# Dots of an attention stage on eight array tiles in two bursts, with maxima per batch and the pad dropped by the exp's bias

## The reference

```python
h = tok(x)                          # windows of 8 time points pooled by a softmax: (128, 94, 64)
h = h + attn(layernorm(h))
h = h + ffn(layernorm(h))           # routed experts, hidden size 128
# attn: 8 heads of 8 features, 94 queries and keys
dots = einsum('bhnd,bhmd->bhnm', q, k)
grass = einsum('bhnd,bhmd->bhnm', qr(q).Q, qr(k).Q) ** 2 * grassman_scale
a = concat([dots * scale, dots ** 2 * riem_scale, grass])      # 24 maps
a = conv_w @ batchnorm(a) + conv_b                             # 8 mixed maps
out = softmax(a, axis=-1) @ v                                  # then the projection
```

## Time and profile before

| | before |
|---|---|
| median of 3 runs | 1039.53 us (1038.96 to 1039.94) |
| profiled execution | 1039.8 us |
| its span | 1038.1 us |
| mean granted TensorE clock | 0.941 |
| PE busy | 919.1 us (89%) |
| DVE busy | 760.2 us (73%) |
| POOL busy | 500.9 us (48%) |
| ACT busy | 400.7 us (39%) |

### The profile page before, as it was taken

The page is one execution under the profiler, slowest core; times in us unless marked ns, Lnnn a source line. Parts: engine busy times, 40 slices in busy tenths (PEclk is TensorE's granted clock), DMA queues, the critical chain, the costliest instruction groups (busy, mean ns, idle before and its releaser), DMA issues. The chain is left out here.

```text
span 1038.1 us, 38252 instructions
## 1 busy us (share of the span) xinstructions
PE 919.1 (89%) x15147; PEld 599.2 (58%) x15147; DVE 760.2 (73%) x1336; ACT 400.7 (39%) x647; POOL 500.9 (48%) x567
## 2 busy tenths in 40 slices
PE   4677678998929999999999999999999998889995
PEld 2233245555626666666666666666666665557673
DVE  4588964887965888888888888888888888645552
ACT  2333422113604444444444444444444443224442
POOL 3355631110026666666666666666666663023440
PEclk8788888998968999999999999999999999889997
DMA  8665000325001111111111111111111110000111
GB/s 302 250 224 193 1 0 4 60 53 134 0 19 53 52 51 51 51 51 50 48 48 47 49 48 51 49 51 51 51 51 51 51 47 23 1 0 21 33 33 33
DMA packets 64446, 63.25 MB, mean 61 GB/s; under 512 B 37081, under 2 KB 55068, under 8 KB 64412
## 3 DMA queue, kind: packets, MB, share of 16 engines
q1 hardware_dynamic: 63884, 61.25, 20.1%
q10 hardware_dynamic: 528, 1.54, 0.4%
HBM read 52.93 MB, written 6.75 MB: 57 GB/s over the span
## 5 line engine op out<-in xcount | busy, mean ns | idle before, releaser
L1177 ACT ACTIVATE sq<-ps_dot 128x752 f32<-128x752 f32 x192 | 153.1, 797 | 302.5 <-PE ps_dot L1056 302.5
L1056 PE MATMUL ps_dot<-q_st,k_blk 32*64 32x94 f32 x6144 | 169.5, 247 | 3.0 <-POOL k_blk L1016 3.0
L1056 PEld LDWEIGHTS ps_dot<-q_st,k_blk 32*64 32x64 f32 x6144 | 134.4, 133 | 64.6 <-issue 50.0
L1016 POOL TENSOR_TENSOR k_blk<-k_turn,hmask 128x384 f32<-128x384 f32 x64 | 65.5, 1023 | 177.4 <-ACT k_turn L1165 177.4
L1224 DVE TENSOR_REDUCE sums<-prob 128x94 f32<-128x564 f32 x128 | 147.9, 1199 | 2.0 <-ACT prob L1170 2.0
L1020 POOL TENSOR_TENSOR k_mix<-k_cm,cols 128x768 f32<-128x768 f32 x64 | 119.9, 1873 | 0.0
L1002 POOL TENSOR_TENSOR v_blk<-v_rep,vmask 128x384 f32<-128x384 f32 x128 | 106.6, 854 | 6.8 <-PE ps_m L1088 6.8
L1105 PEld LDWEIGHTS ps_a<-q_st,k_mix 64*64 64x64 f32 x3072 | 77.2, 132 | 56.4 <-issue 48.2
L1105 PE MATMUL ps_a<-q_st,k_mix 64*64 64x94 f32 x3072 | 101.0, 250 | 0.8 <-DVE prob L1212 0.8
L1170 ACT ACTIVATE prob<-prob,cols 128x564 f32<-128x564 f32 x128 | 91.1, 758 | 20.4 <-DVE prob L1212 20.4
L1195 DVE TENSOR_REDUCE row_max<-ps_a 128x94 f32<-128x564 f32 x128 | 89.3, 741 | 12.4 <-PE ps_a L1124 12.4
(11 more groups left out here) (222 smaller groups left out, 1419.3 us busy)
## 6 DMA issues: line engine op xcount, KB each, us to landing
v_rep<-v_rows SPq DMA_DIRECT2D x256, 96.0 KB
x_g<-in_x_dram SPq DMA_DIRECT2D x15, 1500.0 KB, 6.6
v_rows<-tok SPq DMA_DIRECT2D x32, 96.0 KB
q_st<-q_cm SPq DMA_DIRECT2D x64, 47.0 KB, 1.8
out_dram<-rows SPq DMA_DIRECT2D x16, 188.0 KB
x_g<-in_x_dram ACTq DMA_DIRECT2D x1, 1500.0 KB, 7.4
top_rows<-tok SPq DMA_DIRECT2D x16, 32.0 KB
top<-top_rows SPq DMA_DIRECT2D x1, 512.0 KB, 3.5
```

Source lines behind the costliest of these rows:

```text
L1016: return pool.tensor_tensor(k_blk[:, a, :, kind], view.unsqueeze(2).broadcast_to([128, NTAU, 4, 8]), k["hmask4"][:].unsqueeze(1).unsqueeze ...
L1056: mm = pe.matmul(ps_dot[64 * hg:64 * hg + 64, (a + g) % 2, b, col:col + N], k_blk[rows, a, 2 * (2 * g + t2) + mi].rearrange("p k h m -> p ...
L1177: act.activation(sq[:, :, :, 2 * g:2 * g + 2, :].rearrange("p mi b t n -> p b mi (t n)"), ps_dot[:, (a + g) % 2, :, 0:4 * N].rearrange("p ...
```

## The change

It does five things, all for `attend`.

1. The dots of mi = 1 go to the other column half (`at = 64 * (hg ^ mi)`), so that eight different 32x64 tiles of the array are used. There are two bursts of 24 matmuls; each fills all four banks of `ps_dot` (one for each batch and mi), three values of t a burst.
2. As the head groups of mi = 1 are now swapped on the partitions, `mix_w` has a second, swapped copy (four more small matmuls in `constants`).
3. The turned keys go to `ps_m`, no longer into `ps_dot`. The order on TensorE changes: both transpositions and both spreads of the maxima stand behind the key turn and ahead of the second burst. The second transposition waits for ScalarE's copy of the turned keys (the same bank). Batch 0 has its maxima in a free part of `ps_a`, batch 1 in `ps_m`.
4. ScalarE, no longer VectorE, adds the constant to the spread maxima (`shift_out`). Its queue is: key copy, two squares (one a batch), two shifts, exp of batch 0, two squares, exp of batch 1.
5. VectorE subtracts batch by batch over all six t. The pad keys of t = 5 are dropped by another bias in the exp (`pad_bias`), so each exp is two instructions, 470 and 94 columns. `sums` has two buffers.

```diff
@@ attend: TensorE
-                if later(i, 1) or g == 2:
-                    pe.wait_ge(s["squared"], 3 * i + g - 1)
-                for t2 in range(2):
+                if half or later(i, 1):
+                    pe.wait_ge(s["squared"], 2 * i + half)
+                for t3 in range(3):
                     for mi in range(2):
                         for b in range(2):
                             for hg in range(2):
                                 rows = slice(64 * b + 32 * hg, 64 * b + 32 * hg + 32)
-                                col = N * (2 * mi + t2)
-                                mm = pe.matmul(ps_dot[64 * hg:64 * hg + 64, (a + g) % 2, b, col:col + N],
-                                               k_blk[rows, a, 2 * (2 * g + t2) + mi].rearrange("p k h m -> p (k h m)"),
+                                at = 64 * (hg ^ mi)
+                                mm = pe.matmul(ps_dot[at:at + 64, b, mi, N * t3:N * t3 + N],
+                                               k_blk[rows, a, 2 * (3 * half + t3) + mi].rearrange("p k h m -> p (k h m)"),
                                                q_st[rows, a, :], start=True, stop=True)
...
             def step(i, a, has_prev, has_prev2, has_next):
                 dots(i, a, 0)
-                if has_prev:
-                    turn_max(i - 1)
-                dots(i, a, 1)
-                if has_prev:
-                    spread_max(i - 1)
-                dots(i, a, 2)
                 if has_next:
                     turn_keys(i + 1, 1 - a)
+                if has_prev:
+                    turn_max(i - 1, 0)
+                    if has_next:
+                        pe.wait_ge(s["kt_out"], i + 2)
+                    turn_max(i - 1, 1)
+                    for b in range(2):
+                        spread_max(i - 1, b)
+                dots(i, a, 1)
                 if has_prev2:
                     attended(i - 2, a, False)
-                    denominators(i - 2, i)
+                    denominators(i - 2, a, i)
@@ attend: ScalarE
+            def shift_out(prev, b):
+                act.wait_ge(s["max_spread"], 2 * prev + b + 1)
+                if later(prev, 1):
+                    act.wait_ge(s["sub_done"], 2 * (prev - 1) + b + 1)
+                act.activation(shift[:, b, :], max_bank(b, slice(0, 128), N), ACT.Identity, bias=k["conv_const"]).then_inc(s["max_out"], 1)
+
+            def exps(prev, a, b):
+                act.wait_ge(s["sub_done"], 2 * prev + b + 1)
+                act.activation(prob[:, a, b, 0:5], prob[:, a, b, 0:5], ACT.Exp, bias=k["conv_const"])
+                act.activation(prob[:, a, b, 5], prob[:, a, b, 5], ACT.Exp, bias=k["pad_bias"][:]).then_inc(s["exp_done"], 1)
...
@@ attend: VectorE
-                dve.tensor_scalar(shift[:].rearrange("p b n -> p (b n)"), ps_m[:, 0:N2], k["conv_const"], None, ALU.add).then_inc(s["shift_done"], 1)
...
-                dve.tensor_tensor(prob[:, a, :, 0:5, :], bass.AP(ps_a[:].tensor, A_AT, [[3 * 512, 128], [B_AT - A_AT, 2], [N, 5], [1, N]]),
-                                  shift[:].unsqueeze(2).broadcast_to([128, 2, 5, N]), ALU.subtract)
...
+                for b in range(2):
+                    dve.wait_ge(s["max_out"], 2 * prev + (b + 1))
+                    dve.tensor_tensor(prob[:, a, b], all_logits(b, [[N, NT], [1, N]]), shift[:, b, :].unsqueeze(1).broadcast_to([128, NT, N]),
+                                      ALU.subtract).then_inc(s["sub_done"], 1)
```

More of the change, by code:

```diff
@@ L229, in _ @@
             step(dve.tensor_tensor(k["hmask4"][:], k["hmask"][:, 0:4], k["hmask"][:, 4:8], ALU.add))
-            step(dve.tensor_scalar(k["pad_col"][:], k["delta"][:, 7:8], PAD_GAP, None, ALU.mult))
+            step(dve.scalar_tensor_tensor(out=k["pad_bias"][:], in0=k["delta"][:, 7:8], scalar=-PAD_GAP, in1=k["conv_const"],
+                                          op0=ALU.mult, op1=ALU.add))
             for b in range(2):
@@ L274, in _ @@
             pe.wait_ge(dve_step, marks["mix_rows"])
-            for quarter, source in enumerate((0, 2, 1, 3)):
-                mm = pe.matmul(ps_t[32 * quarter:32 * quarter + 32, 1, 256:320], k["ident"][:, 32 * source:32 * source + 32], mix_rows[:],
-                               start=True, stop=True)
+            for mi, order in enumerate(((0, 2, 1, 3), (1, 3, 0, 2))):
+                for quarter, source in enumerate(order):
+                    mm = pe.matmul(ps_t[32 * quarter:32 * quarter + 32, 1, 256 + 64 * mi:320 + 64 * mi],
+                                   k["ident"][:, 32 * source:32 * source + 32], mix_rows[:], start=True, stop=True)
             mm.then_inc(pe_step, 1)
@@ L957, in attend @@
         prob = sb("prob", [128, 2, 2, NT, N])
-        sums = sb("sums", [128, 2, N])
+        sums = sb("sums", [128, 2, 2, N])
         inv = sb("inv", [128, N])
@@ L1037, in turn_keys, with dots @@
                 pe.wait_ge(s["m_ready"], i + 1)
-                if later(i, 1):
-                    pe.wait_ge(s["squared"], 3 * i - 1)
-                pe.matmul(ps_dot[:, a, 0, KT_AT:KT_AT + NP], m_blk[:, a].rearrange("p q d -> p (q d)"), k_cm[:, span(i, 1), :],
-                          start=True, stop=True).then_inc(s["kt_done"], 1)
-            def dots(i, a, g):
-                if g == 0:
+                if later(i, 4):
+                    pe.wait_ge(s["out_done"], i - 3)
+                pe.matmul(ps_m[:, KT_AT:KT_AT + NP], m_blk[:, a].rearrange("p q d -> p (q d)"), k_cm[:, span(i, 1), :],
+                          start=True, stop=True, skip_group_check=True).then_inc(s["kt_done"], 1)
+            def dots(i, a, half):
+                if half == 0:
                     pe.wait_ge(q_in[a], 16 * ((i - a) // 2 + 1) if isinstance(i, int) else 8 * (i - a) + 16)
@@ L1151, in _ @@
             steps(pe, step)
-            turn_max(PAIRS - 1)
-            spread_max(PAIRS - 1)
+            for b in range(2):
+                turn_max(PAIRS - 1, b)
+            for b in range(2):
+                spread_max(PAIRS - 1, b)
             attended(PAIRS - 2, 0, False)
-            denominators(PAIRS - 2, None)
+            denominators(PAIRS - 2, 0, None)
             attended(PAIRS - 1, 1, True)
-            denominators(PAIRS - 1, None)
+            denominators(PAIRS - 1, 1, None)
         @block.scalar
@@ L1181, in step @@
                 if has_prev:
-                    exps(i - 1, 1 - a)
+                    act.wait_ge(s["mixed"], 2 * i)
+                for b in range(2):
+                    squares(i, 0, b)
+                if has_prev:
+                    for b in range(2):
+                        shift_out(i - 1, b)
+                    exps(i - 1, 1 - a, 0)
+                for b in range(2):
+                    squares(i, 1, b)
+                if has_prev:
+                    exps(i - 1, 1 - a, 1)
             turned_out(0, 0)
             steps(act, step)
-            exps(PAIRS - 1, 1)
+            for b in range(2):
+                shift_out(PAIRS - 1, b)
+            for b in range(2):
+                exps(PAIRS - 1, 1, b)
         @block.vector
```

133 lines of the change are left out of this document (61 added, 72 removed).

## The result

| | before | after |
|---|---|---|
| median of 4 runs each, same chip | 1039.66 us (1038.96 to 1039.94) | 1108.84 us (1105.61 to 1115.37) |
| ratio, 95% interval | | 1.0674 (1.0618 to 1.0731) |
| span of the profiled execution | 1038.1 us | 1104.1 us |
| mean granted TensorE clock | 0.941 | 0.879 |

A forecast was written before the change was run, and what follows sets the result against it. TensorE and VectorE were taken to hold each other in a ring of 8.85 us per step. The new ring through ScalarE summed to 8.46, −0.39 × 62 = −24 us, giving 1015.5 us, range 986 to 1054.

The forecast's parts named there:

- Nothing elsewhere. POOL's turned keys come earlier: POOL: turned keys come earlier, as the key copy ends near 1.4 us of a step, not 4.62; no cost added.
- copies stay: VectorE: copies of the head maxima unchanged, while its work per step falls from 7.4 to about 7.2 us.
- rival E: TensorE's clock falls during small instructions between dot bursts; a step of 9.4 us, +36, 1076 us; chance 0.06.
- the milder half of E: The part of the clock-fall rival counted inside the range: little time at the lower clock level.
- 0.45 us of gaps: TensorE's forecast idle time among five small instructions between 0.64 and 2.79 us of the new step.
- rival C: Eight tiles don't run at once: 0.02 us per pass stays, a burst is 1.13 us, 1069 us; chance 0.12.
- the pass time of a tile: TensorE: a matmul pass occupies its own tile for 0.09 us, however many tiles run beside it.
- the mis-sized term: Dots on TensorE: with six passes per tile, the next burst could start 0.64 us after the old one, not 0.81.
- TensorE's path: Chain beside the new ring, through second transposition, spreads, burst 2, attended and mixing, to 5.83 us; loses by 0.08.
- rival D: ScalarE's chain of nine instructions and five hand-overs is dearer, 0.03 us each; time stays, 1030 to 1044; chance 0.13.
- Rival B: The ring dissolves, engines slip past each other and VectorE's work alone bounds; −78, 962 us; chance 0.07.
- What would show it: Signs for the forecast: 48-pass bursts about 0.7 us, ScalarE start times, clock 0.98 or more; three signs against.

The follow-up runs named there:

- after_reduce: Changed kernel with VectorE's wide copy of the head maxima rewritten as a reduction over an axis of one element; 1028.19 us, ratio 0.9905.
- before_reduce: Kernel before with the wide copies of the head maxima written as reductions over one element, nothing else; 1045.92 us, ratio 1.0073.
- after_fill_small: Changed kernel, copies kept, plus four idle-time matmuls a step whose results go unused; 1048.53 us, ratio 1.0095.
- four_tiles: Changed kernel with the dots back on four of eight array tiles and both mixing weights alike; 1123.02 us, ratio 1.081.
- keys_late: Kernel before with the key turn moved behind attended and denominators, and its ScalarE copy behind the exps; 1113.36 us, ratio 1.0717.

## Why the prediction was wrong

**The step that failed** is "Nothing elsewhere. POOL's turned keys come earlier", with "copies stay" in the paragraph on VectorE. Both sentences were true of the order and false of the time. I had costed the move of the turned keys at nothing without naming what they would lie beside. All that was needed stood in reach: their new time (from 1.8 us of a step, behind `k_mix`, which ends 1.87 us into a step of before; the key copy was forecast to end at 1.4), their length (1.02), and the copies' new place (about 1.8 to 2.5). `after_reduce` shows the cause, one instruction rewritten for 80 us, and `before_reduce` that the rewritten form is no gain where no POOL instruction runs beside it.

**The clock, rival E,** was given 0.06 and 1076 us. Its mechanism is what made a loss of 11 us (`after_fill_small`) into one of 69, and at 60 us it is dearer than the 36 that I had worked out. The range let in only "the milder half of E", so the measured time fell out of it by this term. It was rated low because the forecast step had 0.45 us of gaps. With the held copy TensorE waited 0.31 + 0.64 = 0.95 us between the two bursts of each step, with the reduction 0.31 + 0.32 = 0.63, and the stage's clock was 0.88 and 1.00. So the chance of E hung on a size that I had taken as fixed. The price per disturbed step follows from the rows: attended burst to denominators 610.11 − 608.17 = 1.94 against 1.00, the second dot burst and the denominators 0.21 and 0.17 more, the mixing burst 0.06, in all 1.38. 60 us are thus about 43 such steps of 62, an estimate; the trace has 41 among its last 59. Two limits: `four_tiles` waited longer still (0.31 + 0.85 + 0.16) and kept 0.96, and `keys_late` waited 1.34 us in each step and kept 1.00, so the sum of the gaps alone doesn't tell the level; and why some steps of one kernel fall and others don't stays open.

**Eight tiles do run together;** rival C is refuted. The same burst cut after 0.35 us and whole, from two windows of the timeline of after:

```profile
643.98 0.58 PE L1068 MATMUL ps_dot<-q_st,k_blk 32*64 32x94 f32 x32
```
```profile
643.98 0.87 PE L1068 MATMUL ps_dot<-q_st,k_blk 32*64 32x94 f32 x48
```

The last of 32 passes starts by 644.33, so they start 0.35/31 = 0.011 us apart or less, half of before's 0.020. Cut earlier, the same timeline holds 8 passes by 644.04, 16 by 644.17 and 24 by 644.25: eight start nearly together, and behind the first sixteen the next eight come every 0.08 us, as the groups of four do in a burst of before. So the pass time of a tile stayed what it was (0.09 in the prediction), which was its argument for eight tiles. The 60 cycles per matmul of the Trainium skill, "TensorEngine Tiling (Array Packing)", section Instruction Overhead, an estimated 25 ns at 2.4 GHz, are not borne out as a distance between starts; by them the burst would be 1.2 us.

But the last 16 passes take 0.87 − 0.58 = 0.29, or 0.018 each, which is before's pace. (In the burst at 607.12, most of it at the lower clock, the groups come every 0.15 us to the end, and there is no slower tail.) That is the mis-sized term: the next burst comes 0.80 us after the first and 0.84 after the second (`after_reduce`), not 0.64. A mechanism for the tail was not shown here. The Trainium skill, "TensorE: Matmul & The Clock Gate", section "Architectural detail: the array is 16× 32×32, not 1× 128×128", gives TensorE's queue 64 entries. My guess is that 32 passes with their weight loads fill it during a wait and the rest are fed at 0.018; no run tested it.

**The rest of the sum held,** which `after_reduce` shows, as it is the step that I had added up. Its key copy starts at 1.38 (1.16 forecast) and its second burst at 2.93 (2.79), late behind the first burst's extra 0.16. The attended burst starts at 3.77 (3.43), mixing at 5.05 (4.72), and the first mixing product at 6.17, where TensorE's path had 5.83 and ScalarE's 5.91. From there to the next step it is 2.51 us, as in before. The squares of the second burst end at 602.76 + 1.15 = 603.91, which is 5.85 against 5.86. So TensorE's path is the longer one and not ScalarE's, by 0.3, where the forecast had it shorter by 0.08. In sum 8.68 for 8.46, 0.22 × 62 = 13.6 us, and 1015.5 + 13.6 = 1029 against 1028.2 measured. ScalarE's prices were right (squares 0.63 for 0.64, exps 0.68 and 0.36, shift 0.34), so rival D fell too; the subtractions took 0.74 for 0.77. Rival B's ring never dissolved. Of the signs under "What would show it" none of the three for being wrong came (bursts over 0.9 us at the full clock, dear exps, late row maxima); the granted clock of 0.98 or more, a sign for being right, did not come either, and it was the one that told.

**The account:** before 1038 to 1040; eight tiles and the new ring with the maxima spread by a reduction that nothing holds, 1025 with fillers and 1028 without; copies held by POOL +24; the clock that falls behind them +60; after 1109. Free plain copies in the new ring were in no run.

## What to carry to other kernels

When an instruction moves in time, the engine that it runs on may be idle and the move still not be free: look what runs beside it at its new place, and whether a SBUF copy on VectorE and an instruction on POOL now overlap. In the trace the sign is one form with different durations (228, 402, 610 and 816 ns here), whose ends follow the other engine's; the cure may be one instruction in a slower form that doesn't take the shared thing. A short wait on TensorE's path should be priced with the clock it may lose, and a few cheap matmuls in the wait tell within one run whether that is so.
